# One visit to the attention accumulator per unit instead of two, with the sum of exponentials taken over eight steps

## The reference

```python
# layer 0: softmax attention, residual, layer norm
Q, K, V = q @ Wq.T + bq, ctx @ Wk.T + bk, ctx @ Wv.T + bv      # 16 heads of 32
att = softmax(Q @ K.T / sqrt(32))
x1 = layernorm(att @ V @ Wo.T + bo + q) * gamma0 + beta0
# layer 1: linear attention, residual, layer norm
Qf, Kf = elu(x1), elu(ctx)
KV = einsum('bnd,bne->bde', Kf, ctx)
Z = 1 / (Qf . sum_n(Kf) + 1e-6)
out = layernorm(x1 + (Qf @ KV) * Z) * gamma1 + beta1
```

## Time and profile before

| | |
|---|---|
| median of 3 runs | 1559.48 us |
| profiled execution | 1558.27 us |
| span | 1556.9 us |
| granted TensorE clock, mean | 0.994 |
| PE busy | 1519.1 us (98%) |
| PEld (weight loads) busy | 1030.1 us (66%) |
| DVE busy | 1210.3 us (78%) |
| ACT busy | 813.5 us (52%) |
| POOL busy | 1091.1 us (70%) |

### The profile page before, as it was taken

One profiled execution on the slowest core, in us unless ns is written; L12 is line 12 of the kernel. 1 busy time (PEld: TensorE's weight loads), 2 busy tenths in 40 slices (PEclk: granted clock), 3 DMA queues, 4 the chain that ended last, 5 costly groups with the idle time before them and its releaser, 6 DMA issues.

```text
span 1556.9 us, 30288 instructions
## 1 busy us (share of the span) xinstructions
PE 1519.1 (98%) x10912; PEld 1030.1 (66%) x10912; DVE 1210.3 (78%) x2401; ACT 813.5 (52%) x1576; POOL 1091.1 (70%) x1009
## 2 busy tenths in 40 slices
PE   7999999999999999999999999999999999999997
PEld 5666767676766767667676767666767676756553
DVE  3687786777787878977877787878787788788878
ACT  1364655545555555565555555656555555565631
POOL 0376676756787787957678877776668877787861
PEclk9999999999999999999999999999999999999999
DMA  8755253443324244153342434334343342520001
GB/s 237 204 154 145 62 171 125 130 120 98 116 88 136 77 124 156 54 146 115 99 113 93 136 92 122 124 91 126 113 127 85 117 114 85 139 64 21 12 23 40
DMA packets 160340, 171.06 MB, mean 110 GB/s; under 512 B 21824, under 2 KB 122176, under 8 KB 160192
## 3 DMA queue, kind: packets, MB, share of 16 engines
q1 hardware_dynamic: 155968, 167.30, 36.3%
q10 hardware_dynamic: 4224, 1.84, 0.5%
HBM read 126.10 MB, written 42.99 MB: 109 GB/s over the span
## 4 chain that ended last, share of the span: by engine, by line
PE 85%; DVE 6%; DMA 3%; issue 3%; POOL 2%; SPq 1%; ACT 1%; ACTq 0%; DVEq 0%; POOLq 0%
PE score L442 15%; PE scoreT L456 14%; PE acc L474 14%; PE misc L515 7%; PE misc L491 7%; PE misc L527 6%; PE misc L504 6%; PE misc L543 6%; PE misc L551 5%; PE acc L481 3%; DVE maxes L744 1%; POOL pair_sum L974 1%; DMA q_stack<-q_dram 1%; PE misc L535 1%; DMA bv_col<-bv_in 1%
## 5 line engine op out<-in xcount | busy, mean ns | idle before, releaser
L617 ACT ACTIVATE p_ring<-scoreT 128x512 f32<-128x512 f32 x1024 | 597.1, 595 | 600.2 <-PE scoreT L456 594.5
L974 POOL TENSOR_TENSOR pair_sum<-p_ring 128x512 f32<-128x512 f32 x512 | 657.7, 1296 | 339.2 <-DVE pair_sum L777 215.3
L744 DVE TENSOR_REDUCE maxes<-score 128x1 f32<-128x512 f32 x1024 | 683.2, 680 | 220.0 <-PE score L442 217.4
L442 PE MATMUL score<-k_stack,q_stack 96*128 96x512 f32 x1024 | 637.8, 624 | 9.7 <-DVE maxes L744 6.1
L456 PEld LDWEIGHTS scoreT<-q_stack,k_stack 104*128 104x128 f32 x2048 | 387.0, 191 | 178.1 <-ACT p_ring L617 96.2
L456 PE MATMUL scoreT<-q_stack,k_stack 104*128 104x256 f32 x2048 | 421.9, 288 | 6.9 <-ACT p_ring L617 3.6
L442 PEld LDWEIGHTS score<-k_stack,q_stack 96*128 96x128 f32 x1024 | 193.1, 189 | 183.1 <-issue 129.9
L474 PE MATMUL acc<-p_ring,v_sb 128*32 128x256 f32 x4096 | 249.3, 384 | 2.5 <-issue 2.5
L474 PEld LDWEIGHTS acc<-p_ring,v_sb 128*32 128x32 f32 x4096 | 120.7, 110 | 87.0 <-issue 4.6
L981 POOL TENSOR_TENSOR pair_sum<-pair_sum 128x512 f32<-128x512 f32 x128 | 165.4, 1292 | 0.0
L504 PE MATMUL misc<-ctxT_sb,wk 128*128 128x512 f32 x256 | 132.9, 604 | 3.4 <-DVE k_low L817 2.0
(11 more groups left out here) (81 smaller groups left out, 1231.8 us busy)
## 6 DMA issues: line engine op xcount, KB each, us to landing
xT_sb<-xT_in SPq DMA_DIRECT2D x62, 512.0 KB, 3.8
k_stack<-k_dram SPq DMA_DIRECT2D x96, 256.0 KB, 4.5
q_stack<-q_dram SPq DMA_DIRECT2D x192, 128.0 KB, 2.6
k_dram<-k_high SPq DMA_DIRECT2D x32, 256.0 KB, 2.1
k_dram<-k_low SPq DMA_DIRECT2D x32, 256.0 KB, 2.1
q_dram<-q_high SPq DMA_DIRECT2D x64, 128.0 KB, 1.7
q_dram<-q_low SPq DMA_DIRECT2D x64, 128.0 KB, 1.9
ctx_nat<-ctx_in SPq DMA_DIRECT2D x32, 256.0 KB, 4.3
```

What stands on the lines that cost most here:

```text
L442: pe.matmul(score[k % 3][:], q_stack[0:SPLIT, unit % NQ, j, t * P:(t + 1) * P], k_stack[0:SPLIT, group_of[unit] % 2 * QUAD + j, h * HALF:( ...
L617: act.activation(p_ring[:, n % NP, h * HALF:(h + 1) * HALF], scoreT[k % 2][:], ACT.Exp, scale=SCALE).then_inc(A["exped"], 1)
L744: dve.reduce_max(maxes[:, unit % 2, t, j, h:h + 1], score[k % 3][:], AX.X).then_inc(V["maxed"], 1)
L974: pool.tensor_tensor(pair_sum[:, place_of_pair(pair), cols], p_ring[:, (n - 1) % NP, cols], p_ring[:, n % NP, cols], ALU.add).then_inc(L[" ...
```

## The change

- `visit` comes once per unit, 16 ticks after the unit's first transposed score, with all eight steps (64 visits), and the denominators are added once, from one sum `exp_sum` over the eight steps. `NP` becomes 9; the exponential that needs a ring slot waits for the visit of the unit before.
- The sum is a running one. The low 512 columns are added on GpSimd (`add_low`, seven times per unit). The high 512 are added on GpSimd for steps 2, 3, 5 and on VectorE for steps 1, 4, 6, 7 (`add_high`), each waiting for the one before it.
- `split_max` writes the high part by a second reduction of the same maxima in place of the CAST; three ticks instead of four.
- The negated mean is gone from `aggregate`; the shift on GpSimd takes the mean and multiplies by -1 in the same operation.
- Context features go in pairs: Relu, Exp and the combination over 256 columns, 64 times instead of 128, in place in `fphi_sb`.
- Any norm may take VectorE's way, by the planner's rule of the earlier end.
- The low parts of Q and K are made one tick after the high parts on VectorE's program. `q_high` and `q_low` have one buffer instead of two; Q chains are at least 6 ticks apart.
- The planner gives a visit tick room for 50, lets a booking spill into the next tick, and has other costs and due times (`TILE_TICKS` 20). In the tick after a visit, norms and features of tiles come ahead of the maximum (VectorE) and of the exponential (ScalarE).

```diff
-    NQ, NP, NO, NX = 3, 8, 19, 3
+    NQ, NP, NO, NX = 3, 9, 19, 3
-    VISIT = 4
-    VISITS = KT * UNITS // VISIT
-    VISIT_AT = LEAD + 13
+    VISIT_AT = LEAD + UT
+    HIGH_ON_POOL = (2, 3, 5)
+    HIGH_ON_DVE = (1, 4, 6, 7)
...
+        def span(k):
+            return 50 if visiting(k) is not None else 14
...
-            if tile >= TILES - KT and ended_on_dve < find(f"shift{norm}", "POOL", scaled + 2, 13):
+            if ended_on_dve < find(f"shift{norm}", "POOL", scaled + 2, 13):
...
-            def visit(v):
-                unit, part = divmod(v, KT // VISIT)
+            def visit(unit):
                 group = group_of[unit]
-                if part == 0:
-                    pe.wait_ge(A["v_kept"], 2 * (group + 1))
-                    if unit > 0:
-                        pe.wait_ge(V["out_scaled"], unit)
-                for s in range(VISIT):
-                    n = VISIT * v + s
-                    kt = n % KT
+                pe.wait_ge(A["v_kept"], 2 * (group + 1))
+                if unit > 0:
+                    pe.wait_ge(V["out_scaled"], unit)
+                for kt in range(KT):
+                    n = KT * unit + kt
...
-                pe.wait_ge(L["quad_low"], v + 1)
-                pe.wait_ge(V["quad_high"], v + 1)
+                pe.wait_ge(L["low_added"], (KT - 1) * (unit + 1))
+                pe.wait_ge(V["high_on_dve"], len(HIGH_ON_DVE) * (unit + 1))
                 for j in range(QUAD):
                     mm = pe.matmul(acc[j * DK:(j + 1) * DK, CH:2 * CH], ones[:, 0:DK],
-                                   pair_sum[:, place_of_pair(2 * v), j * CH:(j + 1) * CH], start=False,
-                                   stop=part == KT // VISIT - 1, ...)
+                                   exp_sum[:, j * CH:(j + 1) * CH], start=False, stop=True, ...)
...
                 if h == 0 and n >= NP:
-                    act.wait_ge(T["weighted"], (n - NP) // VISIT + 1)
-                    act.wait_ge(L["paired"], 2 * ((n - NP) // 2 + 1))
+                    act.wait_ge(T["divided"], (n - NP) // KT + 1)
...
+                    dve.tensor_reduce(parts[:, :, 0:QUAD], maxes[:, u], AX.X, ALU.max,
+                                      negate=True).then_inc(V["max_high"], 1)
-                    dve.tensor_copy(parts[:, :, 0:QUAD], max_row[:]).then_inc(V["max_high"], 1)
...
+            def add_high(unit, kt):                      # VectorE; GpSimd has the like for 2, 3, 5
+                n, cols = KT * unit + kt, slice(HALF, 2 * HALF)
+                before = exp_sum[:, cols] if kt > 1 else p_ring[:, (n - 1) % NP, cols]
+                if kt - 1 in HIGH_ON_POOL:
+                    dve.wait_ge(L["high_on_pool"], len(HIGH_ON_POOL) * unit + HIGH_ON_POOL.index(kt - 1) + 1)
+                elif kt > 1:
+                    dve.wait_ge(V["high_on_dve"], len(HIGH_ON_DVE) * unit + HIGH_ON_DVE.index(kt))
+                elif unit > 0:
+                    dve.wait_ge(T["divided"], unit)
+                dve.wait_ge(A["exped"], 2 * n + 2)
+                dve.tensor_tensor(exp_sum[:, cols], before, p_ring[:, n % NP, cols],
+                                  ALU.add).then_inc(V["high_on_dve"], 1)
...
-                dve.tensor_scalar(neg_mean[:, s, :], mean_var[:, s, 0:1], -1.0, None, ALU.mult)
...
-                pool.tensor_tensor(shift[:, s, :], neg_mean[:, s, :], rstd[:, s, :],
+                pool.tensor_scalar(shift[:, s, :], mean_var[:, s, 0:1], rstd[:, s, :], -1.0, ALU.mult,
                                    ALU.mult).then_inc(L[f"shifted{norm}"], 1)
...
+            def add_low(unit, kt):                       # GpSimd, kt = 1 to 7
+                n, cols = KT * unit + kt, slice(0, HALF)
+                before = exp_sum[:, cols] if kt > 1 else p_ring[:, (n - 1) % NP, cols]
+                if kt > 1:
+                    pool.wait_ge(L["low_added"], (KT - 1) * unit + kt - 1)
+                elif unit > 0:
+                    pool.wait_ge(T["divided"], unit)
+                pool.wait_ge(A["exped"], 2 * n + 1)
+                pool.tensor_tensor(exp_sum[:, cols], before, p_ring[:, n % NP, cols],
+                                   ALU.add).then_inc(L["low_added"], 1)
```

More of the change, by code:

```diff
@@ L197, in take @@
             room[engine][k] = room[engine].get(k, 0) + cost
+        def span(k):
+            return 50 if visiting(k) is not None else 14
         def find(name, engine, k, cost):
-            steps = when.setdefault(name, {})
-            while k in steps or room[engine].get(k, 0) + cost > (26 if visiting(k) is not None else 14):
+            steps, load = when.setdefault(name, {}), room[engine]
+            while k in steps or load.get(k, 0) + cost > span(k) and (
+                    load.get(k, 0) > span(k) - 4 or
+                    load.get(k, 0) + cost + load.get(k + 1, 0) > span(k) + span(k + 1)):
                 k += 1
@@ L207, in book @@
             when[name][k] = tile
-            take(engine, k, cost)
+            rest = max(0, room[engine].get(k, 0) + cost - span(k))
+            take(engine, k, cost - rest)
+            take(engine, k + 1, rest)
             return k
@@ L309, in follow @@
             take("ACT", end, cost[0])
-            take("DVE", end, cost[1])
+            take("DVE", end + (kind in "KQ"), cost[1])
             if kind == "Q" and i > 0:
-                put = send("put_queries", end + 1, i, 2, False)
+                put = send("put_queries", end + 2, i, 2, False)
                 if i < NQ:
```

289 lines of the change are left out of this document (143 added, 146 removed).

## The result

The changed kernel takes 1623.81 us (median of 4 runs, 1620.78 to 1626.02) beside 1559.52 for the kernel before, measured with it: ratio 1.0412 [1.0386, 1.0439]. Faster was forecast; it is 64 us slower, beyond the end of the range, also of the one with the rivals (1497 to 1577).

A forecast was written before the change was run, and what follows sets the result against it. PE was taken as the bound, with DVE having 347 us free. Savings of 15 (first batch), 9 (S stages), 4 (tile stages) and 4 (tail) made 32, from 1558.3 to 1526, said as 1527; range 1512 to 1545, with rivals 1497 to 1577.

The forecast's parts named there:

- The visit tick: On PE, two visit ticks costing 6.30 us per unit become one of eight steps at 4.90 us plus an ordinary tick.
- rival 3: DVE becomes the bound in the tile stages as all norms move and two-operand operations wait for POOL: 1575 us, chance 0.21.
- PE's gain of 60 us: On PE, halving the visits was to save 0.93 us per unit, 60 us in 64 units.
- 87%: PE keeps its 15 us: First batch: DVE needs 268 of 307.7 us, so PE's whole saving of 15 us stays.
- so 12 - 3 = 9 us stay: S stages: DVE needs 252 of 272 us, 93%, and 9 us of PE's saving of 12 stay.
- I allow it 96%: Tile stages: DVE's 796 us at a 96% share make 829 us, so 4 of 33 us stay.
- The unit with 94%: S-stage unit from 606.30 in the kernel before, DVE busy 20.02 of 21.20 us, PE idle 0.42, cited as precedent for 93%.
- up to 0.5 us late: Denominators on PE could start this late after the visit, 32 us over all units at worst; costed at nothing.
- slack of a unit: SP's query stores one tick later and one query buffer, chains 6 ticks apart, were to have this slack; costed at nothing.
- the 0.38 us paid once: Time per visit tick on PE for going into and out of the narrow matmuls, once per unit after the change.
- or if they grow: Sign that the forecast is wrong: the tile stages grow, which would mean that DVE is the bound.
- if PE waits for the sums at the denominators: Sign that the forecast is wrong: PE stands at the denominators for the last sums.

The follow-up runs named there:

- e3: Changed kernel with VectorE's four high sums per unit replaced by a maximum over 32 columns (output not the reference's): 1547.0 us, 0.9928 of the kernel before.
- e14: Changed kernel with two visits of four steps per unit and the denominators one tick after the second: 1598.2 us, 1.0235 of the kernel before.
- e11: Changed kernel with the denominators' matmuls one tick after the visit and normalise a tick later: 1624.3 us, 1.0415 of the kernel before.
- e2: Changed kernel with VectorE's high sums replaced by a maximum over all 512 columns, one SBUF operand (output not the reference's): 1579.4 us, 1.0129 of the kernel before.
- e1: Changed kernel with norms before the last batch back on GpSimd and ScalarE: 1593.5 us, 1.0222 of the kernel before.
- e15: Changed kernel with denominators one tick later and VectorE's high sum of step 6 two ticks later, in the visit's tick: 1617.7 us, 1.0367 of the kernel before.
- e12: Changed kernel with the low parts of Q and K again in the tick of the high parts: 1632.4 us, 1.0491 of the kernel before.
- e6: Changed kernel with high sums reading 32 columns (output not the reference's) and norms before the last batch on GpSimd and ScalarE: 1550.5 us, 0.9929 of the kernel before.
- e8: Kernel before with only the smaller VectorE operations: second reduction, no negated mean, paired context features, one low query buffer: 1552.9 us, 0.9944 of the kernel before.
- after: The changed kernel itself, as measured beside the kernel before: 1623.81 us, ratio 1.0412.
- e10: Kernel before, two visits kept, with denominators once per unit from one sum and the smaller VectorE operations: 1540.5 us, 0.9889 of the kernel before.

## Why the prediction was wrong, step by step

**What held.** The visit tick: 4.90 us forecast, median 4.985. The kinds of work and their sum on DVE: 1390 forecast, 1374.7 measured. In it the high sums cost 0.99 and not 1.10 each (252.7 us for 282), the norms 2.02 and not 2.35 (60.2 + 44.6 us over 52), the context features 0.94 and not 0.75 (60.3 for 48), and the second reduction 0.155 in place of the CAST's 0.53, as forecast. DVE's waits for ACT's high parts fell from 77 to 5.6 us (keys; none is left for queries). Two sizes were off in the count: 38 norms moved, not 29, more than the 31 from which rival 3 was to decide; and PE's gain of 60 us, of which e3's PE shows 31.3 in busy time (1519.1 to 1487.8). PE's waits for DVE's maxima, forecast at some 80 us, are 135.6 (93.5 + 42.1).

**The step that failed** is the one from DVE's busy time to the length of a stage: "87%: PE keeps its 15 us" in the first batch, "so 12 - 3 = 9 us stay" in the S stages and "I allow it 96%" in the tile stages. The measured shares are 81, 85 to 87, and 86 to 89%, all below what was allowed, and every one of these stages grew. A stage's share is a mean over ticks of two kinds. In eleven ticks of sixteen DVE has hardly any idle time; in the visit it has no scores, because, as I read it, one visit of 4.98 us is longer than the work that the three score banks hold for it (3 x 0.68; no run changed their number). What DVE can't do in the visit is room lost, and the full ticks then run at DVE's pace, with PE idle in them: its idle time per unit is 1.35 us instead of 0.18, 1.06 of it outside the visit's tick. The unit with 94% was no proof to the contrary: it had two short visits, and its room lay spread over the unit. e14 against e11 gives a size: nearly the same work with the visit halved is 26 us faster, about 21 without the 6 norms. e3, e2 and e1 show the other side, and e3 and e2 more firmly, since they change nothing but the high sums: with less work for DVE, 77, 44 and 30 us come back, and PE's own waits for the maxima fall from 42.1 to 14.9, 24.4 and 30.3 us. So it is shown that DVE's added work costs the loss at shares of 81 to 89%; that the pattern of full and starved ticks is the way is supported by the tick table and e14, but argued, and e15 doesn't bear it out.

**Missing terms.** PE's gaps cost clock: some 20 us of the loss, at most 23 (28 against 8 and 32 against 9, above), are not the gaps but the slower pieces behind them; the prediction had no such term. This is an estimate from the granted clock; no run took the clock alone away. PE's wait at the denominators, called "up to 0.5 us late" and counted at nothing, is 0.28 us per unit, 18 us; what it cost is open, as e11 paid for its removal. DVE's wait in `add_high` for GpSimd's part, counted at nothing too, is 10.5 us in ten waits (L802's line above). The queries' "slack of a unit" was wrong by little: PE waited 10.2 us for q_stack's loads, 2.9 before, and 6.4 with the low parts at once (e12).

**The two rules weighed.** High sums: by the Trainium skill ("SBUF — State Buffer", Who interferes with whom), the later of the two instructions waits for the whole of the other, which gave 1.13 for each. The mean of 0.99, beside e2's 0.673 with one operand, sides with waiting and not with the bare 0.68. For the worst case a wait for one other instruction is too short: e6 shows six operations of POOL beside one of DVE. By another rule of the Trainium skill ("TensorEngine Tiling (Array Packing)", Key Properties) a change of the tiling mode drains TensorE. The visit tick's median of 4.985 us, which was summed with the 0.38 us paid once, agrees with it, and so do e11's ticks 10 and 11, which grew with a second way in; no run took the drain away by itself.

**The rivals.** Rival 3 had the mechanism (DVE becomes the bound) and a tell ("or if they grow") that came true, as did "if PE waits for the sums at the denominators". But it was priced by the same average (1575, or 1605 with dear sums), and put into the tile stages alone, while 28 of the 64 us (some 24 at equal numbers of pieces) lie in the first batch and the S stages.

**What stays open.** With DVE relieved (e3, e6) the changed kernel still gains only some 10 of 60 us, and part of that may be the smaller operations' (e8). In e3 PE's busy time fell by 31.3 us while its idle time rose from 37.8 to 56.7. By stages, the tile stages rose by 20.5 us (3.1 to 23.6) and the first batch by 6.2 (4.8 to 11.0, 8.4 of which are waits for the loads of queries and keys); the S stages and the tail fell. In the tile stages PE waits for several things of DVE, the maxima (10.2 us) and the features of tiles (5.3) above all, and the granted clock is at 0.98 to 1.00; stalls like e6's are rare. The other 29 of the 60 us may be time that the records, with modelled ends, don't show as idle before either; no run separates it. In e14 the first batch is 337.9 us, longer than after's 330.4, with DVE at 78%. The ticks show where: its two visits and the denominators (ticks 2, 10 and 11) together take 8.06 us per unit there (units 3 to 15), against 7.07 in after, and the other thirteen gave back 0.56. PE goes into the narrow matmuls three times per unit in e14 and once in after; in this stage, with DVE at 78%, the one long visit was the cheaper way.

## What to carry to other kernels

Read an engine's room between its waits, tick by tick, and not from its share of a stage: here shares of 81 to 89% left hardly any room in eleven of sixteen ticks. A longer block on the bound engine can starve whoever feeds on it for as long as the buffers between don't reach, and that engine's work then lands, late, in ticks that were already full. So a merged block wants its additions paid for where they land: e10 kept the visits short, took the denominators once, and made room on VectorE by the smaller operations first. And an idle gap on the bound engine can be paid a second time, in a slower clock behind it (12 times in this kernel, with 29 gaps of more than 1 us).

## What the hardware showed unexpectedly

A DVE operation with two operands in SBUF can stand behind several GpSimd operations, not only one: 7.64 us for L900 in e6 across six operations of 1.25 to 1.28 us, and 6.66 us for L784, an operation on 128x8 elements with a median of 0.34, beside the same kind of row. That it is the access to SBUF they wait for is read from the records lying side by side; no run took it away for them alone. A reduction with one SBUF operand paid no such wait beside the same sums on POOL; the single line of e2 (duration ns least/median/most):

```profile
L803 DVE TENSOR_REDUCE probe<-p_ring x256: 644/674/687, 58.3 to 1531.5; 128x1 f32<-128x512 f32 x128
```

Of 256 none took longer than 0.687 us, where the high sums of the changed kernel have a mean of 0.99. After a PE gap of 2.22 us the same piece took 1.52 and 1.91 us, at a granted clock of 0.64 and 0.59, before it was back at 1.02.
